# Attention on one Trainium2 core: two PSUM banks for the latents and one for the weighed values, with the weighing done in every step

## The reference

```python
q = _rmsnorm(x @ wq_a.T, q_a_ln_w) @ wq_b.T          # 32 heads, 64 plain + 64 rope
ckv, k_pe = (x @ wkv_a.T)[..., :64], (x @ wkv_a.T)[..., 64:]
kv = _rmsnorm(ckv, kv_a_ln_w) @ wkv_b.T
q_pe, k_pe = _apply_rope(q_pe), _apply_rope(k_pe)
scores = einsum('bqhd,bkhd->bhqk', q_full, k_full) * softmax_scale   # causal
attn = softmax(scores, axis=-1)
out = einsum('bhqk,bkhd->bqhd', attn, v).reshape(B, S, H * VD) @ wo.T
```

## Time and profile before

| | |
|---|---|
| median of 3 runs | 2439.2 us (2436.16 to 2441.24) |
| profiled execution | 2439.96 us, its span 2438.3 us |
| attention, 905 to 1582 us | 677 us, TensorE busy 648.19, VectorE 582.04, ScalarE 607.09, GpSimd 466.26 |
| before it, 0 to 905 us | 905 us, TensorE busy 849.78 |
| after it, 1582 to 2438 us | 856 us, TensorE busy 828.38 |
| granted TensorE clock, mean of each of the three | 0.98, 0.98, 0.99 |

### The profile page before, as it was taken

How to read it: one execution, slowest core, us unless ns; L and a number is a source line. 1 busy time by engine, 2 the same in 40 slices (tenths; PEclk the granted TensorE clock), 3 DMA queues, 4 the chain that set the end, 5 groups by cost and what they waited for, 6 DMA issues and landing times. The chain is left out here.

```text
span 2438.3 us, 45823 instructions
## 1 busy us (share of the span) xinstructions
PE 2326.4 (95%) x14640; PEld 2038.1 (84%) x14640; DVE 1811.2 (74%) x3542; ACT 1240.9 (51%) x3724; POOL 1218.7 (50%) x1012
## 2 busy tenths in 40 slices
PE   8999999988899979999999999899999998999998
PEld 6888888866577758999999999788888877899998
DVE  8987777776467758989898989655776575777775
ACT  5566554442355549999999999732332223111110
POOL 5667776673023336677767776510676553111110
PEclk9999999999999989999999999899999999999999
DMA  7774567777466740111111112296888988122121
GB/s 247 242 233 147 180 214 255 241 241 273 147 214 229 229 143 17 57 52 47 51 56 51 45 51 68 69 327 195 241 250 238 290 271 270 53 70 70 69 69 52
DMA packets 319400, 382.00 MB, mean 157 GB/s; under 512 B 23680, under 2 KB 227968, under 8 KB 319104
## 3 DMA queue, kind: packets, MB, share of 16 engines
q1 hardware_dynamic: 311472, 352.30, 45.8%
q0 software_dynamic: 7184, 25.69, 2.7%
q10 hardware_dynamic: 576, 2.10, 0.3%
HBM read 297.68 MB, written 81.80 MB: 156 GB/s over the span
## 5 line engine op out<-in xcount | busy, mean ns | idle before, releaser
L1537 ACT ACTIVATE attn_prob<-attn_prob,attn_bias 94x94 f32<-94x94 f32 x1024 | 366.7, 361 | 45.8 <-DVE attn_bias L1613 44.3
L670 DVE TENSOR_TENSOR up_t_lo<-early_raw,up_t_hi 128x512 fp32r<-128x512 f32 (+1 forms) x210 | 221.0, 1056 | 120.1 <-ACT up_t_hi L596 117.8
L538 POOL TENSOR_TENSOR early_raw<-early_raw 128x512 f32<-128x512 f32 (+1 forms) x150 | 231.9, 1551 | 142.5 <-DMA early_raw<-x_f 82.3
L1658 POOL TENSOR_TENSOR attn_prob<-attn_prob,attn_share 94x752 f32<-94x752 f32 x128 | 188.3, 1471 | 177.5 <-DVE attn_share L1621 177.5
L1913 POOL TENSOR_TENSOR early_raw<-early_raw 128x512 f32<-128x512 f32 x120 | 170.2, 1423 | 199.9 <-DMA early_raw<-o_t 199.5
L1963 DVE TENSOR_TENSOR out_t_lo<-early_raw,out_t_hi 128x512 fp32r<-128x512 f32 x168 | 159.6, 954 | 139.5 <-ACT out_t_hi L1927 138.7
L596 ACT ACTIVATE up_t_hi<-early_raw 128x512 fp32r<-128x512 f32 (+1 forms) x210 | 130.4, 622 | 258.2 <-POOL early_raw L538 179.6
L1927 ACT ACTIVATE out_t_hi<-early_raw 128x512 fp32r<-128x512 f32 x168 | 105.0, 631 | 307.6 <-POOL early_raw L1913 155.9
L734 PE MATMUL up_ps<-up_t_lo,early_s_hi 128*128 128x512 f32 (+1 forms) x616 | 241.1, 391 | 12.8 <-DVE up_t_lo L670 12.8
L735 PE MATMUL up_ps<-up_t_hi,early_s_lo 128*128 128x512 f32 (+1 forms) x616 | 239.1, 388 | 0.0
L736 PE MATMUL up_ps<-up_t_hi,early_s_hi 128*128 128x512 f32 (+1 forms) x616 | 238.9, 388 | 0.0
(11 more groups left out here) (267 smaller groups left out, 6628.2 us busy)
## 6 DMA issues: line engine op xcount, KB each, us to landing
early_raw<-o_t SPq DMA_DIRECT2D x288, 256.0 KB, 4.9
early_raw<-x_f SPq DMA_DIRECT2D x240, 256.0 KB, 3.9
shared_ring<-w SPq DMA_DIRECT2D x120, 256.0 KB, 4.0
early_raw<-x_f SPq DMA_DIRECT2D x120, 240.0 KB, 4.0
shared_ring<-wvo SPq DMA_DIRECT2D x96, 256.0 KB, 4.9
o_t<-attn_o_t SPq DMA_DIRECT2D x128, 188.0 KB, 1.9
shared_ring<-wo SPq DMA_DIRECT2D x32, 512.0 KB, 6.7
y<-early_raw POOLq DMA_DIRECT2D x24, 512.0 KB, 3.6
```

What stands on the lines that cost most here:

```text
L538: nc.gpsimd.tensor_tensor(both[n % 2][:, 0:w], a, b, SEVEN[i].op_b).then_inc(both_done, 1)
L670: nc.vector.tensor_tensor(t_lo[s % NT][:, 0:w], src, t_hi[s % NT][:, 0:w], ALU.subtract).then_inc(lo_done, 1)
L1537: last = nc.scalar.activation(prob[u % NPR][0:SEQ, h, part], prob[u % NPR][0:SEQ, h, part], ACT.Exp, bias=bias[u % 2][0:SEQ, n:n + 1], sca ...
L1658: nc.gpsimd.tensor_tensor(p4, p4, share[u % 2][0:SEQ, :].unsqueeze(2).broadcast_to((SEQ, 8, SEQ)), ALU.mult).then_inc(prob_done, 1)
```

## The change

The bank that `ps_o` gives up goes to `ps_l`, which becomes a list of two, used in turn by even and odd steps. The latents' product of item j then waits for ScalarE's copies of item j-2. The weighed block loses its loop over two distances: it stands in every step, for the item five steps old, and waits for the copy of the item before it. The copy out of `ps_o` comes at distance 6. The numbers of matmuls, copies and transfers stay the same, and so does the order on VectorE, ScalarE and GpSimd but for the item that the copy takes. Line numbers move by one or two.

```diff
--- before.py
+++ after.py
@@ -1320,11 +1320,11 @@
         prob_t = [mem.sb(f"prob_t{i}", [P, 2, GT]) for i in range(NPT)]
         o_t = [mem.sb(f"o_t{i}", [P, GT]) for i in range(2)]
         zero = mem.sb("zero", [P, PAIRS, TOKP - TOK])
-        ps_l = mem.ps("ps_l", [P, 512])
+        ps_l = [mem.ps(f"ps_l{i}", [P, 512]) for i in range(2)]
         ps_r = mem.ps("ps_r", [P, 512])
         ps_s = mem.ps("ps_s", [P, 2, 512])
         ps_t = mem.ps("ps_t", [P, 2, 512])
-        ps_o = [mem.ps(f"ps_o{i}", [P, 512]) for i in range(2)]
+        ps_o = mem.ps("ps_o", [P, 512])
         ps_v = [ps_s[:, 0, :], ps_s[:, 1, :], ps_t[:, 0, :], ps_t[:, 1, :]]
         w_in = mem.sems("w_in", 2)
         w_hi_done = mem.sem("w_hi_done")
@@ -1360,8 +1360,7 @@
         N = PAIRS * GROUPS
         U = 2 * GROUPS
 
-        D_S, D_N, D_T, D_O = 1, 2, 4, 8
-        D_V = (7, 6)
+        D_S, D_N, D_T, D_V, D_O = 1, 2, 4, 5, 6
         DEPTH = D_O
         PREP = 4
 
@@ -1425,9 +1424,12 @@
                     if g == 0:
                         pe.wait_ge(w_lo_done, 4 * kb + (2 * w + 2))
                     cols = slice(GT * g, GT * g + GT)
-                    for ps, at, sem, free in ((ps_r, P, rope_made, swap_done), (ps_l, 0, latent_made, latent_done)):
-                        if not first(j, 1):
-                            pe.wait_ge(free, j)
+                    for ps, at, sem in ((ps_r, P, rope_made), (ps_l[u % 2], 0, latent_made)):
+                        if ps is ps_r:
+                            if not first(j, 1):
+                                pe.wait_ge(swap_done, j)
+                        elif not first(j, 2):
+                            pe.wait_ge(latent_done, j - 1)
                         for c in range(2):
                             wh, wl = w_hi[w][:, c, at:at + P], w_lo[w][:, c, at:at + P]
                             nc.tensor.matmul(ps[:, 0:GT], wl, qn_hi[:, c, cols], start=(c == 0), stop=False)
@@ -1464,21 +1466,20 @@
                             last = nc.tensor.transpose(ps_t[0:SEQ, h, part], prob[u % NPR][0:SEQ, h, part],
                                                        ident[0:SEQ, 0:SEQ])
                     last.then_inc(turned, 1)
-                for back in D_V if m % 2 == 1 else ():
-                    s = stage(k, m, back, U, N)
-                    if s is not None:
-                        j, u, kb = s
-                        g = u % GROUPS
-                        pe.wait_ge(prob_t_done, j + 1)
-                        if not first(j, 2):
-                            pe.wait_ge(o_done, j - 1)
-                        for b in range(GB):
-                            for h in range(2):
-                                last = nc.tensor.matmul(ps_o[u % 2][64 * h:64 * h + 64, SEQ * b:SEQ * b + SEQ],
-                                                        v[0:96, GB * g + b, :],
-                                                        prob_t[u % NPT][0:96, h, SEQ * b:SEQ * b + SEQ],
-                                                        start=True, stop=True)
-                        last.then_inc(weighed, 1)
+                s = stage(k, m, D_V, U, N)
+                if s is not None:
+                    j, u, kb = s
+                    g = u % GROUPS
+                    pe.wait_ge(prob_t_done, j + 1)
+                    if not first(j, 1):
+                        pe.wait_ge(o_done, j)
+                    for b in range(GB):
+                        for h in range(2):
+                            last = nc.tensor.matmul(ps_o[64 * h:64 * h + 64, SEQ * b:SEQ * b + SEQ],
+                                                    v[0:96, GB * g + b, :],
+                                                    prob_t[u % NPT][0:96, h, SEQ * b:SEQ * b + SEQ],
+                                                    start=True, stop=True)
+                    last.then_inc(weighed, 1)
 
             run_steps(pe, N, DEPTH, U, body, at=0)
 
@@ -1505,8 +1506,8 @@
                     act.wait_ge(latent_made, j + 1)
                     if not first(j, 2):
                         act.wait_ge(scored, j - 1)
-                    nc.scalar.activation(q_a[u % 2][0:64, :], ps_l[0:64, 0:GT], ACT.Copy)
-                    nc.scalar.activation(q_b[u % 2][64:P, :], ps_l[64:P, 0:GT], ACT.Copy).then_inc(latent_done, 1)
+                    nc.scalar.activation(q_a[u % 2][0:64, :], ps_l[u % 2][0:64, 0:GT], ACT.Copy)
+                    nc.scalar.activation(q_b[u % 2][64:P, :], ps_l[u % 2][64:P, 0:GT], ACT.Copy).then_inc(latent_done, 1)
                     if first(j, 1):
                         values_and_keys()
                     for c in range(2):
@@ -1581,7 +1582,7 @@
                     dve.wait_ge(weighed, j + 1)
                     if not first(j, 2):
                         dve.wait_ge(o_stored[u % 2], 16 * bodied(0, kb, u, 2))
-                    nc.vector.tensor_copy(o_t[u % 2][:], ps_o[u % 2][:, 0:GT]).then_inc(o_done, 1)
+                    nc.vector.tensor_copy(o_t[u % 2][:], ps_o[:, 0:GT]).then_inc(o_done, 1)
                 s = stage(k, m, D_S, U, N)
                 if s is not None:
                     j, u, kb = s
```

## The result

The changed kernel takes 2445.68 us (median of 8 runs, 2442.3 to 2448.76) against 2438.22 (8 runs, 2435.79 to 2441.44) for the kernel before, run beside it: a ratio of 1.003, 95% interval 1.002 to 1.004. It is slower by 0.3%. The forecast was 2446.5, slower by 0.27%. That figure is for the profiled execution, which took 2446.72.

The account below looks back on a forecast made before the run. TensorE was taken to bound the attention stage except at stalls. 602.1 + 17.8 - 607.5 = +12.4 us for 119 steps, -0.5 and -5.4 at the ends, gave +6.5 on 2439.96: 2446.5, 8-in-10 range 2431 to 2454.

Parts of the forecast that it names:

- The step of 5.06: TensorE's attention step when weighing every step: 3.52 + 0.74 + 0.80 us, a pair 10.12 in place of 9.78.
- the price of a drain: Cost of TensorE changing tiling mode around the weighed block, put at 0.34 us per pair of steps.
- The weighed block's waits: TensorE waits for VectorE's ps_o copy behind the weight split: 1.04 or 1.50 us per eight steps, 17.8 in all.
- upper bound of 24.9: Most the weighed block's waits could cost, in us, if lags add up in both split steps of all groups.
- Rival B: Faster: VectorE starts early enough that the weighed block does not wait for its copy; 2428.7 us, chance 0.13.
- Part 1: Two latents' banks: the product waits for an older ScalarE copy, so all that wait goes, at most 25.5 us less.
- 25.5 us of stalls: TensorE's stalls over 119 attention steps: 607.5 us measured against 582 at its own pace of 9.78 per pair.
- The rule to rotate through banks: Skill rule that independent groups rotate through banks so copying out overlaps; said to favour two latents' banks, oppose one weighed-values bank.
- part 3: One bank for weighed values, one step sooner: each block waits for VectorE's copy, behind the weight split; 17.8 us lost.
- Ends: Attention's first eight steps, -0.5 us, and its emptying after step 127, from 29.0 to 23.7 to 24.1, taken as -5.4.

Follow-up runs that it names:

- e9: The changed kernel with the weight split moved to the end of VectorE's step: 2427.31 us, ratio 0.9954.
- e7: The changed kernel with the old banks (one for latents, two for weighed values) and the weight split at the end of VectorE's step: 2428.49 us, ratio 0.9963.
- e6: The kernel before with the weight split moved to the end of VectorE's step, behind the reciprocal: 2422.44 us, ratio 0.9937.
- e1: The changed kernel with the old banks, one for latents and two for weighed values, still weighing every step: 2442.08 us, ratio 1.0021.
- e2: The changed kernel with VectorE's copy out of ps_o put ahead of its weight split: 2428.05 us, ratio 0.9957.
- e3: The changed kernel with one bank for the latents in place of two: 2447.74 us, ratio 1.0043.
- e8: The changed kernel with VectorE's copy ahead of the weight split and one bank for the latents: 2430.98 us, ratio 0.9971.
- e5: The kernel before with VectorE's copy of the weighed values put ahead of the weight split: 2425.55 us, ratio 0.9949.
- e4: The changed kernel with weighing and storing one step later (D_V 6, D_O 7): 2448.35 us, ratio 1.0036.

## Why the prediction was right, point by point

**The step of 5.06** measured 5.045 (40.36 for the eight steps of e9's groups), 119 x 0.015 = 1.8 us less than forecast. Its size was right because it was a sum of pitches between rows. The pair takes 10.09, 0.31 over the 9.78 of before, where 0.34 was forecast; the prediction calls this the price of a drain, and no run separates a drain from what else entering the block costs. The effect of weighing every step is e7 against e6, both with the split last and in the old banks: the loop 601.11 against 593.11, 8.0 longer, and 2428.49 against 2422.44, 6.0 in all. With the split where it was it is e1 against before: the loop 8.2 longer, a ratio of 1.0021, 4 to 5 us in all. So weighing every step costs 8 us of loop and 4 to 6 in all, wherever VectorE's split stands.

**The weighed block's waits**: 1.04 and 1.50 per group were forecast; groups of eight take 41.45 and 41.83 against 40.36 without waits, so 1.09 and 1.47. Over the loop, 618.63 - 119 x 5.045 = 18.3 against 17.8. The single steps fit as well. With an output weight's split ahead they take 5.90 and 5.66, so 0.86 and 0.62 are lost where 0.90 and 0.60 were forecast; without it 5.52 and 5.66, so 0.48 and 0.62 for 0.44 and 0.60. (The prediction's upper bound of 24.9 uses a 0.88 for which it gives no working; the forecast does not rest on it.) Rival B, that VectorE would be early enough, was refuted by those two rows, and e2 shows what it would have given: 2428.05, where B said 2428.7.

**Part 1, the latents' second bank.** "All of this wait goes" is true of the trace, yet the cause given fails: with one bank (e3) it goes from the loop as well. Nor is it only that TensorE stands at the weighed block and gives ScalarE its time: in e7 it never waits at the weighed block, there is one latents' bank, and no matmul of the loop waits for the latents' copy. What takes the wait away is a short split together with even steps; with the uneven steps of e6 some of it stays. Of the 25.5 us of stalls that the forecast removed, 14.4 went in e6 with the split's place alone (25.5 to 11.1), and of the 18.3 that came in their place all but 0.3 went so in e9. To that extent the two are one thing, VectorE late after a long split, paid in two places. Where e6's remaining 11.1 come from stays open. The rule to rotate through banks, which the prediction takes from the Trainium skill, Perfetto Trace Analysis, Matmuls, is worth 0.2 us of loop in the changed kernel (e3) and 2.9 with the copy first (e8 against e2).

**The step that failed** is the reading of the earlier trace rows in part 3: "the split starts 0.95 after the first reader and holds 1.71". The number was right and the forecast stood on it, but I took it for the price of a subtraction. Its own price is 0.41; the rest is waiting for GpSimd, whose rows stood beside it. This did no harm to the forecast, since the change leaves the split where it meets GpSimd. One more row of that group could have told it: a 128x512 subtraction, with twice the elements, took 0.69, less than half of the 128x256 one.

**Ends.** Steps 0 to 7 gained nothing (+1.07 against -0.5). Step 1 alone took 8.72 against 7.50. It took 7.50 in e9 too and 8.10 to 8.73 in the eight others, e5 and e6 with before's banks and depths among them, so it isn't the change's. The emptying was 24.99, with 23.7 to 24.1 forecast. Two things were missing: a wait of 0.59 of the scores for VectorE's rope sum, and 0.6 in the last two blocks. (The sum took -5.4, but the prediction's own 23.7 to 24.1 give -5.3 to -4.9.) Each took 1.57 and 1.56 from its start to its copy's (1588.76 and 1591.01), where I had 1.25, the pitch of blocks that follow one another:

```profile
1574.67 0.87 PE L1454 MATMUL attn_ps_s<-shared_k_t,attn_q_a 128*94 128x94 f32 x8 [0.59 <-DVE attn_q_b L1602]
...
1587.19 1.52 PE L1478 MATMUL attn_ps_o<-attn_prob_t,attn_v 96*64 96x94 f32 x16
1589.45 1.52 PE L1478 MATMUL attn_ps_o<-attn_prob_t,attn_v 96*64 96x94 f32 x16 [0.74 <-DVE attn_o_t L1585]
```

How much the change shortens the emptying isn't shown. e5 and e6, with the depths of before, take 24.91 and 26.12. The 29.04 of the profiled run of before held a wait of 2.99 for a store, and e5's trace has no such wait at the last copy. In the same banks e7 has 24.11 against e6's 26.12. One step more of depth cost 2.2 us (e4, one trace).

**Not forecast**: the rest of the program, untouched, was 2.80 us shorter after. Over the eleven traces it is 850.8 to 854.8. The kernels with one bank for the weighed values have 851.2, 851.4, 851.4, 852.3, 850.8 and 854.7; those with two have 853.6 to 854.8. No run separates a cause, so it stays open. Errors of -1.3 in the loop, +1.6 and +1.4 at the ends, +1.5 ahead and -2.8 behind add up to +0.3 of the span: the total came out that close partly by luck.

## What to carry to other kernels

Before a step is priced by a row, hold that row against a similar one: an operation far longer than another of twice its size may be waiting for something that no list of waits names. Here, moving it away from what it waited for was worth more than rearranging whoever waited for it. The whole question of banks and of weighing every step was worth 2 to 8 us, and a few lines moved on VectorE 12 to 18. When one late engine feeds two waits, taking away one of them can move the cost to the other, as in e1, so ask first whether both have the same source.

## What the runs showed of the hardware

A VectorE subtraction with both inputs in SBUF, 128x256, takes 0.41 us alone and up to 1.87 when GpSimd's two multiplies run one behind the other: it ends 0.27 to 0.29 behind the second, in all 224 cases of the eight traces. The rope sum, also with two inputs in SBUF, behaves alike (0.53 alone, up to 1.37). The copy and the mask, which read PSUM, keep their 0.53 and 0.92 beside the same GpSimd work. The time of standing is shown as busy time of the one that stands, not as a wait. The Trainium skill, SBUF — State Buffer, SBUF: two separate sides, says that VectorE and GpSimd share one pair of ports, taken as an exclusive lock by whoever comes first, and that a VectorE operation with two SBUF inputs needs it while GpSimd reads SBUF. The lengths of 1766, 1318 and 410 ns agree. The page has no figure for it: that the split stands could have been suspected from it and the rows of before, and its own 0.41 is first measured in e6.
